# A two-layer graph kernel: one branch a tile in TensorE's last loop, XW made in two bf16 parts, and the work before the loop reordered

## What is computed

```python
# layer 0
deg = clip(adj.sum(1), 1);  dis = deg ** -0.5
sim = x @ x.T / (norms[:, None] * norms[None, :])
attn = softmax(beta * sim * adj, axis=1)
x = layernorm(x + (dis * adj * dis) @ x - x + sigmoid(alpha) * (attn @ x - x))
# layer 1
XW = x @ W
s_col = XW @ a[:128];  s_row = XW @ a[128:]
den = exp(leaky_relu(s_row[:, None] + s_col[None, :], 0.01))
num = adj @ den
att = where(num != 0, den / num, 0)
x = layernorm(x + adj @ (att @ XW))
```

## Time and profile before

| what | us |
|---|---|
| median of 3 runs | 726.48 |
| lowest and highest run | 725.94, 730.57 |
| the profiled execution | 728.87 |
| its span in the trace | 727.1 |
| loop of layer 1 in the span | 433.6 to 646.0 |

### The profile page before, as it was taken

How to read it: one execution, slowest core, us unless ns; L and a number is a source line. 1 busy time by engine, 2 the same in 40 slices (tenths; PEclk the granted TensorE clock), 3 DMA queues, 4 the chain that set the end, 5 groups by cost and what they waited for, 6 DMA issues and landing times.

```text
span 727.1 us, 11809 instructions
## 1 busy us (share of the span) xinstructions
PE 596.3 (82%) x4179; PEld 345.3 (47%) x4179; DVE 576.3 (79%) x1043; ACT 445.5 (61%) x689; POOL 388.7 (53%) x456
## 2 busy tenths in 40 slices
PE   5499999999998779999526978878889878787994
PEld 5243333333332668888423643333444333345883
DVE  2589999999999863688786768887988988995442
ACT  2388888888888332679964227876766777741000
POOL 5458888877778224456207154464564543001764
PEclk9999999999999589999656998999999999997998
DMA  9964444490000000000000032233332322100110
GB/s 146 101 68 39 39 39 39 51 379 31 1 1 0 6 0 15 23 17 16 17 0 23 14 110 52 83 88 88 88 88 65 81 70 81 43 4 3 31 30 15
DMA packets 17841, 37.94 MB, mean 52 GB/s; under 512 B 2570, under 2 KB 8222, under 8 KB 17726
## 3 DMA queue, kind: packets, MB, share of 16 engines
q0 software_dynamic: 7392, 24.32, 19.6%
q1 hardware_dynamic: 10334, 11.98, 5.0%
HBM read 48.72 MB, written 10.45 MB: 81 GB/s over the span
## 4 chain that ended last, share of the span: by engine, by line
PE 34%; DVE 25%; issue 21%; POOL 12%; ACT 5%; DMA 1%; DVEq 0%; POOLq 0%; ACTq 0%; SPq 0%
DVE ring L825 8%; PE PSALL L1633 8%; DVE R L834 7%; PE PSALL L1388 5%; POOL AW L459 5%; PE PSALL L1501 3%; ACT AW L608 3%; PE PSALL L1618 3%; PE PSALL L1369 2%; POOL X L472 2%; PE PSALL L1319 2%; PE PSALL L1583 2%; POOL X L450 2%; PE PSALL L1447 1%; POOL iota L470 1%
## 5 line engine op out<-in xcount | busy, mean ns | idle before, releaser
L398 POOL TENSOR_TENSOR R<-R,ring 128x452 f32<-128x452 f32 (+1 forms) x126 | 151.6, 1204 | 33.2 <-ACT ring L536 31.5
L834 DVE SCALAR_TENSOR_TENSOR R<-ring,R 128x452 bf16<-128x452 f32 (+1 forms) x132 | 134.7, 1021 | 0.0
L1369 PE MATMUL PSALL<-R,AO 128*128 128x452 bf16 (+2 forms) x396 | 99.3, 360 | 16.1 <-DVE R L834 15.0
L459 POOL DMA_INDIRECT AW<-ATd,FR x44 | 50.4, 1146 | 106.9 <-PE PSALL L1585 81.7
L536 ACT ACTIVATE ring<-ring,sm 128x452 f32<-128x452 f32 (+1 forms) x132 | 88.4, 670 | 27.8 <-DVE ring L825 21.0
L1319 PE MATMUL PSALL<-XN 128*128 128x452 f16 (+2 forms) x396 | 99.3, 362 | 4.7 <-issue 4.2
L1583 PE MATMUL PSALL<-AW,R 128*128 128x452 fp8e4 x348 | 89.6, 359 | 7.2 <-DVE R L1167 3.7
L544 ACT ACTIVATE R<-ring,sm 128x452 bf16<-128x452 f32 (+1 forms) x132 | 88.6, 671 | 4.3
L1618 PE MATMUL PSALL<-ring,X 128*128 128x452 bf16 (+1 forms) x300 | 69.2, 366 | 19.5 <-issue 14.0
L825 DVE TENSOR_TENSOR ring<-PSALL,AT 128x452 f32<-128x452 f32 (+1 forms) x132 | 81.0, 614 | 0.9 <-PE PSALL L1319 0.9
L1369 PEld LDWEIGHTS PSALL<-R,AO 128*128 128x128 bf16 (+1 forms) x396 | 28.5, 97 | 76.2 <-DVE R L834 62.0
(11 more groups left out here) (256 smaller groups left out, 1033.6 us busy)
## 6 DMA issues: line engine op xcount, KB each, us to landing
AT<-in_adjT POOLq DMA_DIRECT2D x22, 338.5 KB, 6.5
ATd<-AT SPq DMA_DIRECT2D x2, 3723.5 KB, 17.3
XWd<-ring SPq DMA_DIRECT2D x11, 128.0 KB, 1.8
out<-ring SPq DMA_DIRECT2D x21, 64.0 KB, 1.5
AW<-ATd,FR POOLq DMA_INDIRECT x44
X<-XWd,idx POOLq DMA_INDIRECT x22, 3.8
Wt<-in_W SPq DMA_DIRECT2D x1, 64.0 KB, 10.8
X<-in_x SPq DMA_DIRECT2D x1, 0.5 KB, 7.6
```

Of the source, the lines that this page charges most:

```text
L398: i = G.tensor_tensor(ES_, ES_, z, ALU.add)
L459: G.indirect_dma_start(out=AW2[:, jt % 3, q, :], out_offset=None, in_=ATd, in_offset=bass.IndirectOffsetOnAxis(ap=idxw[:, q, jt:jt + 1], a ...
L834: V.scalar_tensor_tensor(F[0:rows, RW:RW + w], z, 1.0, F[0:rows, 0:w], ALU.subtract, ALU.subtract).then_inc(s_low, 1)
L1369: m = TE.matmul(PSALL[:, c, 0:w], half_[0:rows, jt, :], F[0:rows, o:o + w], start=(jt == 0 and k == 0), stop=(jt == T - 1 and k == 2))
```

## The change

*The loop.* TensorE takes one branch a tile. Each of the three branch bodies holds the tile's three units for one kind, with their products (`tile`, `xw_product`); the kinds are told apart by If and Else. The products of the last three units stand behind the loop.

*XW in two parts.* ScalarE writes the high bf16 half of XW when it copies it out of PSUM, VectorE the rest (`xw_low`), and XWd holds both, so that the fetched rows are ready for use. GpSimd's `split_xw` is gone. The column sums of an iteration of layer 0's spread now stand before its `xw_part`.

*Last row sums.* For the steps (1, 20), (1, 21) and (0, 21) one VectorE instruction compares against all keys, masks by `onesU` and adds up the row itself. ScalarE has no row sum for these, and `rows_no` counts those it has.

*Diagonals and order.* ScalarE makes the 22 blocks of `cdiag` by scaled copies of the identity. The steps of kind 0 stand later on VectorE, and column sums, `spread_c`, `block_sums` and `empties` stand in another order on TensorE. `empties` uses two more banks, and VectorE's `table` and `without_empty` are ordered accordingly.

```diff
+XWb4 = [half_.bitcast(BF16).rearrange("p (t c d) -> p t c d", t=2, c=2) for half_ in XWb]
...
-XWh = X[:, :].bitcast(BF16).rearrange("p (t d c) -> p t d c", t=T, c=2)
+XWh = X[:, :].bitcast(BF16).rearrange("p (t c d) -> p t c d", t=T, c=2)
...
+OWN_SUM = {(1, T - 2), (1, T - 1), (0, T - 1)}
...
+def rows_no(n):
+    return sum(s not in OWN_SUM for s in STEPS[:n])
...
-OBANK, CBANK = (6, 4), (2, 3, 4, 5, 2, 3)
+OBANK, CBANK, EBANK = (6, 4), (2, 3, 4, 5, 2, 3), (6, 7, 6, 7, 0, 1)
...
+    G.memset(onesU[:, 0:NP - P], 1.0).then_inc(s_ones, 1)
+    G.tensor_copy(onesU[:, NP - P:NP], U[:, :]).then_inc(s_ones, 1)
...
-    def split_xw(t):
...
-        G.tensor_copy(iota[:, :], XWs[:, t, :]).then_inc(s_xws, 1)
-        gp.wait_ge(s_xws, 3 * t + 1)
-        G.tensor_tensor(XWh[:, t, :, 0], XWs[:, t, :], iota[:, :], ALU.subtract).then_inc(s_xws, 1)
-        gp.wait_ge(s_xws, 3 * t + 2)
-        G.tensor_copy(XWh[:, t, :, 1], iota[:, :]).then_inc(s_xws, 1)
...
-    for g, (t0, nb) in enumerate(GRP):
-        G.tensor_tensor(cdiag[g][:, 0:nb * P].rearrange("p (t j) -> p t j", t=nb),
-                        ident[:, :].unsqueeze(1).broadcast_to([P, nb, P]),
-                        c99[:, t0:t0 + nb].unsqueeze(2).broadcast_to([P, nb, P]), ALU.mult).then_inc(s_cdiag, 1)
...
-    for jt in range(2):
+    for jt in range(T):
...
-    for t in range(2):
-        split_xw(t)
-    for jt in range(2, T):
-        if jt + 4 < T:
+        if jt >= 2 and jt + 4 < T:
             fetch_xw(jt + 4)
-        split_xw(jt)
-        fetch_rows(jt)
...
-            S.activation(XWb[h], PSALL[:, 4, 256:256 + w], ACT.Copy).then_inc(s_xwc, 1)
+            S.activation(XWb4[h][:, :, 1, :], PSALL[:, 4, 256:256 + w].rearrange("p (t d) -> p t d", t=nb), ACT.Copy).then_inc(s_xwh, 1)
...
-    for t in range(T - 5, T):
+    for t in range(T - 5, T - 2):
         row_sum(1, t)
-    for t in (T - 5, T - 4):
-        row_sum(0, t)
+    row_sum(0, T - 5)
     av.wait_ge(s_padr, 1)
     S.activation(l_w, srow, ACT.Exp, scale=SLOPE).then_inc(s_lexp, 1)
     av.wait_ge(s_lexp, 1)
     S.activation(lhl[:, 0, :], l_w, ACT.Copy).then_inc(s_lexp, 1)
-    row_sum(0, T - 3)
+    row_sum(0, T - 4)
+    def diagonal(t0, t1):
+        for t in range(t0, t1):
+            av.wait_ge(s_c99, 1)
+            S.activation(cdiag[t // 4][:, t % 4 * P:(t % 4 + 1) * P], ident[:, :], ACT.Copy, scale=c99[:, t:t + 1]).then_inc(s_cdiag, 1)
+    diagonal(0, 4)
...
     S.activation(sU, sU, ACT.Exp).then_inc(s_eU, 1)
-    row_sum(0, T - 2)
+    diagonal(4, T)
...
+    def spread_out(g):
+        t0, nb = GRP[g]
+        av.wait_ge(s_cball, g + 1)
+        S.activation(cb[:, t0 * P:(t0 + nb) * P], PSALL[:, CBANK[g], 0:nb * P], ACT.Copy).then_inc(s_cbc, 1)
...
+    row_sum(0, T - 3)
     av.wait_ge(s_wU, 1)
     S.activation(w88[:, :, 0:T], wU, ACT.Copy).then_inc(s_whi, 1)
-    row_sum(0, T - 1)
-    for g, (t0, nb) in enumerate(GRP):
-        av.wait_ge(s_cball, g + 1)
-        S.activation(cb[:, t0 * P:(t0 + nb) * P], PSALL[:, CBANK[g], 0:nb * P], ACT.Copy).then_inc(s_cbc, 1)
+    spread_out(0)
+    spread_out(1)
+    row_sum(0, T - 2)
+    for g in range(2, 6):
+        spread_out(g)
     reg = {}
...
+    def xw_low(g):
+        h = g % 2
+        dv.wait_ge(s_xwh, g + 1)
+        V.tensor_tensor(XWb4[h][:, :, 0, :], PSALL[:, 4, 256:512].rearrange("p (t d) -> p t d", t=2), XWb4[h][:, :, 1, :],
+                        ALU.subtract).then_inc(s_xwc, 1)
...
+            if (kind, t) in OWN_SUM:
+                dv.wait_ge(s_ones, 2)
+                dv.wait_ge(s_rkset, 2)
+                V.scalar_tensor_tensor(Cb[n % 3][0:rows, 0:lo + P], key[0:rows, 0:lo + P], sc1, onesU[0:rows, NP - P - lo:NP],
+                                       ALU.is_le, ALU.mult, accum_out=racc[kind][0:rows, t:t + 1]).then_inc(s_less, 2)
+                continue
...
+        if it >= 5 and it % 2:
+            xw_low((it - 5) // 2)
...
-    rank_steps([(1, t) for t in range(T - 5, T)])
+    xw_low(9)
+    rank_steps([(1, t) for t in range(T - 5, T - 2)])
+    xw_low(10)
+    rank_steps([(1, T - 2), (1, T - 1)])
+    dv.wait_ge(s_key, len(PAIR))
...
-    rank_steps([(0, T - 4)])
...
     hots(1)
     valued(1, thirds(1))
     places(1)
-    rank_steps([(0, T - 3)])
+    rank_steps([(0, T - 4)])
...
-    rank_steps([(0, T - 2)])
...
     dv.wait_ge(s_padr, 3)
     for q in range(2):
         V.tensor_tensor(w88[:, :, (2 + q) * T:(3 + q) * T], mLU[:, :, 0:T], per_node(lhl[:, q, :]), ALU.mult).then_inc(s_w88, 1)
+    rank_steps([(0, T - 3)])
     dv.wait_ge(s_whi, 1)
     V.tensor_tensor(w88[:, :, T:2 * T], wU, w88[:, :, 0:T], ALU.subtract).then_inc(s_w88, 1)
+    rank_steps([(0, T - 2)])
     rank_steps([(0, T - 1)])
     V.scalar_tensor_tensor(e_bias, above_all, is_u, own_tile, ALU.mult, ALU.add).then_inc(s_ebias, 1)
...
-        for part, g in behind.get(it, []):
-            xw_part(part, g)
         if it >= 7:
             for kind in range(2):
                 col_sums(kind, it - 7)
+        for part, g in behind.get(it, []):
+            xw_part(part, g)
...
-    col_sums(0, T - 4)
...
-        pe.wait_ge(s_cdiag, g + 1)
+        pe.wait_ge(s_cdiag, t0 + nb)
...
     ordered(1)
-    col_sums(0, T - 3)
+    col_sums(0, T - 4)
...
-    col_sums(0, T - 2)
+    spread_c(0)
     pe.wait_ge(s_mask, 2)
...
-    for g in range(4):
+    for g in range(1, 4):
         spread_c(g)
+    col_sums(0, T - 3)
     block_sums(0)
+    col_sums(0, T - 2)
+    spread_c(4)
+    spread_c(5)
+    block_sums(1)
     col_sums(0, T - 1)
-    for g in (4, 5):
-        spread_c(g)
-    block_sums(1)
     both_parts(0)
     block_sums(2)
     both_parts(1)
     ordered(0)
     block_sums(3)
     both_parts(2)
+    empties(0)
+    empties(1)
     block_sums(4)
     both_parts(3)
-    empties(0)
-    empties(1)
     block_sums(5)
+    empties(2)
+    empties(3)
     both_parts(4)
     both_parts(5)
-    for c in range(2, NC):
-        empties(c)
...
+    empties(4)
+    empties(5)
+    def num(v, kind):
         jt, s = v // 3, T + v // 3 % 2 * DS
...
+        for h in range(2):
+            b, (c0, w) = 6 + h, CH[2 * (v % 3) + h]
+            if v:
+                pe.wait_ge(s_ln, 2 * v - 1 + h)
+            if kind < 2:
+                for q in range(kind + 1):
+                    for part in (1, 0):
+                        TE.matmul(PSALL[:, b, 0:w], den_h[:, s + 1 + q, :, part], AW[:, jt % 3, q, c0:c0 + w],
+                                  start=(q == 0 and part == 1), stop=False)
+                m = TE.matmul(PSALL[:, b, 0:w], den_h[:, s, :, 1], tab[:, c0:c0 + w], start=False, stop=True)
+            else:
+                for t in range(T):
+                    for part in (1, 0):
+                        m = TE.matmul(PSALL[:, b, 0:w], den_h[:, t, :, part], AT[:, t, c0:c0 + w],
+                                      start=(t == 0 and part == 1), stop=(t == T - 1 and part == 0))
+            m.then_inc(s_num, 1)
+    def xw_product(p):
+        jt, high, lower = p // 3, *halves_of(p)
+        pe.wait_ge(s_alo, p + 1)
+        pe.wait_ge(s_AT[jt], 32)
+        for q in range(2):
+            c = 2 * (p % 3) + q
+            part_of = slice(q * RW, q * RW + CH[c][1])
+            for k, (part, att) in enumerate(((1, high), (1, lower), (0, high))):
+                m = TE.matmul(PSALL[:, c, 0:CH[c][1]], XWh[:, jt, part, :], att[:, part_of],
+                              start=(jt == 0 and k == 0), stop=(jt == T - 1 and k == 2))
+        m.then_inc(s_y, 1)
+    def tile(jt, kind):
+        for v in range(3 * jt, 3 * jt + 3):
+            num(v, kind)
+            if v >= LAG:
+                xw_product(v - LAG)
+    pe.wait_ge(s_win, WIN)
+    for jt in range(T):
+        kind_of = eng.value_load(win[0:1, jt:jt + 1], min_val=0, max_val=2)
         pe.wait_ge(s_denb, 2 * (jt + 1))
         pe.wait_ge(s_AW[jt % 3], 16 * WN * (jt // 3 + 1))
         pe.wait_ge(s_rbm, NC)
         pe.wait_ge(s_tab, NC)
...
         met = pe.covered()
...
+        with eng.If(kind_of == 0):
+            tile(jt, 0)
         pe.only(met)
...
+        with eng.Else():
+            with eng.If(kind_of == 1):
+                tile(jt, 1)
+            pe.only(met)
+            with eng.Else():
+                tile(jt, 2)
+            pe.only(met)
+    for p in range(NV - LAG, NV):
+        xw_product(p)
     for g, (t0, nb) in enumerate(GRP):
```

More of the change, by code:

```diff
@@ L114, in adj_resnorm2_kernel @@
         U = sb("U", [P, P], BF16)
+        onesU = sb("onesU", [P, NP], BF16)
         ones = sb("ones", [P, 1], BF16)
@@ L1194, in _ @@
             den_scores(0)
+            without_empty(0)
+            without_empty(1)
             table(0)
@@ L1205, in _ @@
             table(3)
+            table(4)
+            table(5)
             without_empty(4)
             without_empty(5)
-            table(4)
-            table(5)
             def attention_scores(v):
@@ L1515, in empties @@
                 pe.wait_ge(s_tabs, 5)
-                if c >= 2:
```

(68 more changed lines are left out.)

29 lines of the change are left out of this document (11 added, 18 removed).

## The result

| kernel | median of its runs, us | ratio to before, 95% interval |
|---|---|---|
| before (4 runs) | 727.25 | |
| changed (4 runs) | 763.75 (759.46 to 767.71) | 1.049 (1.041 to 1.058) |

The change makes the kernel 5% slower. The prediction was 710, with a range of 698 to 728 and 0.08 for slower. Its profiled execution took 767.69; the four were 759.46, 759.81, 767.69 and 767.71.

The account below looks back on a forecast made before the run. TensorE's loop was taken as starved of instructions (30.9 us of issue waits), with VectorE bounding narrow tiles afterwards. 728.87 - 15 (loop) - 1 (before it) = 712.9, less 2.4 for the runs' median: 710.5, rounded to 710; range 698 to 728.

Parts of the forecast that it names:

- The long steps: Layer 1 loop, each tile's end: sequencer steps over 330 or 282 matmuls of unwanted bodies; taken as hidden, cost 0.
- What shows of it: Visible cost of the step at each tile's end: taken as 0, possible from 0 to 2.4 us.
- The step's price: Tile's end in the loop: branch, read of the kind and further branches, 4.5 us from the last instruction queued.
- 23 matmuls must stand queued: Tile's end in the loop: TensorE needs 23 matmuls queued to hide the step.
- 30 behind its first products: Narrow tile in the loop: 30 matmuls stand behind its first products, against the 23 needed to hide the step.
- queue of about 16: Rival: each tile's end shows 1.4 us, loop -5, kernel 720; shares 0.16 with the other rival near 720.
- long steps show: Rival: queue takes twelve matmuls only, each tile's end shows 2.4 us, loop 229.1, kernel 742; chance 0.08.
- Their break-even of 1.6: Visible time per tile's end at which the forecast loop passes the 212.4 us of before.
- The pieces that end just behind a landing: Loop: code pieces ending just behind where the step lands, in one narrow tile in four; 2 us over the loop.
- VectorE as the bound: Loop: VectorE sets narrow tiles at 8.4 us (floor 8.2), TensorE kind 1 at 9.4; loop 197.3, -15.
- What was won is handed back: Before the loop: block sums start 4 us earlier, but settle(0) comes later and ordered(0) ends as now; 0.
- The rule on the queue: TensorE's queue of 64 places: 32 matmuls with weight loads, 6.2 us, would hide the long step whole.

Follow-up runs that it names:

- the near step: Changed kernel without the code for tiles of kind 2, so a tile's end steps over 48 matmuls instead of 330; 720.20 us, ratio 0.989.
- the fastest kernel: Changed kernel with transposed rows in bank 7, loop written twice, tile 21's column sums earlier, layer 0's column sums behind XW's parts again; 700.00 us, ratio 0.961.
- the old loop: Changed kernel with the loop of before on TensorE (three If blocks a unit), everything else of the change kept; 739.37 us, ratio 1.017.
- the comparison above: Loop stage with GpSimd's splits (kernel before with only the loop written twice, 710.75 us) beside the one without (the fastest kernel, 700.00 us).
- the rows in bank 7: Changed kernel with the transposed rows of a pair of tiles in PSUM bank 7 instead of bank 4; 749.00 us, ratio 1.027.
- The reads at 670.8 to 678.0: Kernel before with four register reads put into the final products, to measure the sequencer's lead over the array; 728.57 us, ratio not given.

## Why the prediction was wrong

The loop was put at 197.3 and took 235.3. The long steps are worth 45 of it where 2 were put down; without them the loop took 190.0 where the prediction's terms give 195.3. Before the loop, -1 was forecast and +16 came.

**The term that failed most** is "What shows of it ... I take 0, as 16 were seen without a sign of a limit". The step's price was right: 4.5 us from the last instruction queued, and the trace after has 4.4 (561.6 to 566.0). (Its parts were misread a little: the packet of the earlier trace rows is asked for 1.1 to 1.25 us after the branch at 572.7, not 0.9; the sum, 3.46, stands.) That 23 matmuls must stand queued was right too. But at a read the lead was 16 each time, so the long lead seen before, at 505.0, was as long as any that was measured there. And a narrow tile never has "30 behind its first products" queued at its branch, because the branch is taken only after the last wait is met, and then only 12 are left. The prediction counted the instructions behind the tile's first wait, where it had to count those left when its last is met. What the rivals "queue of about 16" and "long steps show" had, 1.4 and 2.4 us a tile end, was measured: mostly 1.3 to 1.6 in tiles of kind 1 and 1.9 to 2.5 in narrow ones. Their break-even of 1.6 no run tests.

**Two terms were missing behind it.** Even "long steps show" gave 229 for the loop and it took 235.3. The pieces that end just behind a landing cost more than the 2 us taken (5.8 in the worst tile), and the stalls cost 13 us of clock, for which no term stood at all, though the earlier trace rows has a clock of 0.52 in a stretch where TensorE mostly waited.

**VectorE as the bound** was right where the step is short: 190.0 with the near step and 189.1 in the fastest kernel for a stage that was put at 197.3, with VectorE idle for 14 us of the first (some 15 were forecast). The gain of the new form was even undersized: 20 us where 15 was forecast.

**XW in two parts** was costed "at nothing", covered by TensorE's matmuls. The durations were right (0.42 for a subtraction, 0.35 forecast), but the added wait was not followed: who frees bank 4 changed from ScalarE, at once, to VectorE, behind two comparisons. That was 14 of the 16 us before the loop. The prediction asked what the subtraction costs VectorE, and not who waits for it.

**GpSimd's splits** were costed at nothing too, "none on the path". In the old loop, where they went too, the stage took 2.8 less (209.6 against 212.4); in a loop that VectorE bounds they cost some 4, as far as the comparison above goes.

**Last row sums** were put at -1.5, and one profile has 1.6. Yet with the rows in bank 7 settle(1) only stood where it was: something took the gain back. The moved column sums, costed at nothing, are the likeliest (settle(1) comes 1.5 earlier without them); the subtractions have no run of their own. **Diagonals**: the masks went to 0.66 each as said; block sums started 12.25 behind c's values (c99; 393.71 to 405.96) instead of 15.44, -3.2 for -4; settle(0) came 11.2 behind them, forecast 11.3. "What was won is handed back" held, and a little more was lost, with TensorE standing 3.12 us for the sorting and then running it at half clock (0.50).

**The rule on the queue.** The prediction weighed the Trainium skill's 64 places ("Advanced Engine Details and Errata", Engine Queue Depths) against the 16 matmuls that the trace showed, and took the view that the queue would hold enough, as the rule has it. The reads at 670.8 to 678.0 show a lead of 32 instructions, with no sign of 64. The measurement decides. The lines of 16 KB for 256 instructions that the Trainium skill has on the same page (ISA Cache) agree with the packets, 16.4 KB each. The Trainium skill says "Only 2 cache lines!" there, but gives TensorE 128 KB, which would be eight; each piece of this loop is run through once, so no run tells how many fit. What was seen is that a step over 48 matmuls took under 0.4 in the kernel with the near step, and one over 282 or 330 took 3.2 to 4.5.

## What to carry to other kernels

Code that is stepped over isn't free: here a step over 564 or 660 instructions, with the read behind it, cost TensorE some 4.5 us before the next matmul, and in the kernel with the near step one over 96 took 0.4 at most. Rarely used bodies belong out of the loop that runs, chosen once by a flag. Whether such a wait is hidden is read from what the array still has to run when the last late semaphore is met, not from the length of the straight code, and from a measured lead. When a read of a buffer moves to another engine, follow who waits for that buffer, in the order of the new engine's queue.

## What the runs showed of the hardware

At a register read TensorE's sequencer was 16 matmuls with their weight loads ahead of the array, four times out of four. It started a tile's branch 0.06 to 0.13 us after the last wait was met, at all 21 tile ends, and never before. Kernels with long steps scatter more (741.72 to 752.68, 747.91 to 757.75, 759.46 to 767.71) than those with short ones (718.80 to 721.58, 704.97 to 706.78), in four runs each; the kernel before lies between (725.12 to 732.68 in eleven on one chip). Each kernel with long steps has some 20 fetches on its path, and where a gap grew to 5.8 us the clock fell to half behind it. That the scatter comes from there is likely, but no run separates it.
